# Attention heads of a fused transformer kernel: who splits the negated maxima and who normalises the outputs

## The chip, the cores and the metric

One NeuronCore of a Trainium2 chip runs the whole program. The metric is the device time of one execution, in microseconds (us). The engines are TensorE (PE, matrix products and transpositions), VectorE (DVE), ScalarE (ACT), GpSimd (POOL) and SyncE (SP, which issues transfers).

## What is computed

The program is two transformer layers with a layer norm behind each block. The change touches only the first attention, on 4 sequences of 1024 rows of 128, with 16 heads of 8 columns:

```python
q = split_heads(embedding @ Wq + bq)
k = split_heads(embedding @ Wk + bk)
v = split_heads(embedding @ Wv + bv)
scale = 1.0 / np.sqrt(HDIM)
scores = jnp.einsum('bhqd,bhkd->bhqk', q, k) * scale
attn = jax.nn.softmax(scores, axis=-1)
av = jnp.einsum('bhqk,bhkd->bhqd', attn, v)
```

The softmax needs the maximum of every row of scores. Behind it stand a projection with a norm, a window attention with two layers and feed-forward blocks, a second attention and a last feed-forward block; they are about 1300 of the 2100 us and stay as they are.

## The kernel before

`phase_l0_heads` works in 32 **units**: a unit `n` is one head and one half `z` (512 query columns) of all 4 sequences. Every unit has 8 groups `g` of 128 keys, and every group two half steps `k`. Three units are in work at once:

- For unit `n + 2` (`after2`), TensorE forms plain scores (`cross`, line 433), 32 tiles of 128 rows by 512 columns a unit, two in each half step, into a ring of three PSUM banks `pX`. VectorE takes the maximum of each (`top`, L554) and folds the two halves of each row together with a change of sign (`fold`, L559) at the unit's end. The result `neg` is 128 x 16.
- For unit `n + 1` (`after`), TensorE transposes `neg` in group 1 (`turn_neg`, L441) into a bank of the same ring. `split_neg` writes it as two bf16 rows, the rounded value (L566) and the remainder (L568), and SyncE stores them as two more rows of the operand `Q`, so that the score product of the unit subtracts the maximum.
- For unit `n`, TensorE forms the scores transposed, less the maximum (`score_and_cross`, L448), into two PSUM buffers `pS`; ScalarE takes the exponential (L537); TensorE multiplies by the values (`products`, L465, eight of 32 x 256 a half step) into the one buffer `pO`, with a column of ones that gives the sum.
- For unit `n - 1` (`before`), ScalarE copies `pO` to `O` in group 1 (`take_sums`, L530), TensorE transposes it at the end of group 3 (`close`, L476, four transpositions, again in a bank of the ring), and `norm` on VectorE takes reciprocals of the sums (L576) and multiplies (L580).

Order on each engine is the order of the code, and all dependencies are semaphores. TensorE forms two `cross` tiles beside the two score tiles of each half step, on different rows of the array, and then products. The ring decides how far it runs ahead of VectorE: class `Banks` hands out the three banks in turn; the second number that `take` returns, `back`, says how many maxima may still be missing when a bank is written again. Since VectorE read the transposed tiles in its own order, one counter, `topped`, freed all banks. The first products of a unit wait until `O` has been copied (`o_ready`), since `pO` is single.

The first two units' maxima are formed before unit 0. The loop over units 1 to 24 is a hardware loop of 8 units, taken three times; units 25 to 31 are written out. Units 30 and 31 have no maxima to form. GpSimd only copied values for a head to come (L417). The next phase, `phase_project_norm`, starts behind a barrier of all engines.

## Time and profile before

| | |
|---|---|
| time of 3 runs, median (lowest to highest) | 2095.55 us (2095.2 to 2096.95) |
| the profiled execution, time / span | 2095.52 us / 2093.5 us |
| heads, from the first maximum to the last product of `norm` | 64.4 to 777.6 us |
| PE / DVE / ACT / POOL busy, of the span | 80% / 80% / 56% / 33% |
| the same from 300 to 400 us, within the heads | PE 97.3, DVE 98.2, ACT 81.3, POOL 0.8 of 100 us |
| granted clock of TensorE from 300 to 400 us | 1.00 (2.4 GHz) |

A row of a timeline merges equal instructions that follow each other; the length of such a row is from its first start to its last end. An instruction of an engine may start before the one ahead has ended. A matmul's end is modelled. "Idle before" is the engine's idle time ahead of the row, with the instruction that ended it.

### The profile page before, as it was taken

The page shows a single profiled execution, that of the slowest core. Times are in us where ns is not written, and L with a number is a line of the kernel's source. Part 1 is how long each engine was busy: PE and PEld are TensorE (multiplying, and loading weights), DVE is VectorE, ACT ScalarE, POOL GpSimd, SP SyncE. Part 2 cuts the span into 40 slices and gives each one's busy share as a digit, 9 for nine tenths or more (in the row PEclk, how much of TensorE's full clock was granted, in tenths as well). Part 3 has the DMA queues.
Part 4 walks back from the last instruction along what each step waited for, and adds up shares of the span by engine and source line. Part 5 has one row for each costly group of instructions (what it writes and reads, how often), then busy time and mean ns, then how long its engine had stood idle before and what let it go on. Part 6 is the DMA issues. An engine that isn't in the chain of part 4 may idle for free. (4 is left out here: it accounts for less than half of the span.)

```text
span 2093.5 us, 47784 instructions
## 1 busy us (share of the span) xinstructions
PE 1681.3 (80%) x15985; PEld 891.1 (43%) x15985; DVE 1676.9 (80%) x3448; ACT 1169.1 (56%) x2316; POOL 697.4 (33%) x531
## 2 busy tenths in 40 slices
PE   5799999999999983788888595888885752676768
PEld 3123322323232323455555362655554432565645
DVE  6799999999999916799999464999995778677546
ACT  4078878877888871577777322777775210332411
POOL 3000000000000003788888224888884333223101
PEclk9589999999999996999999897999998975887879
DMA  5200000000010004000000222000001231010022
GB/s 167 62 8 26 17 18 22 27 18 17 20 29 2 2 16 126 16 20 20 22 19 17 56 81 68 21 20 22 19 19 42 77 87 30 2 30 21 22 73 70
DMA packets 144154, 75.92 MB, mean 36 GB/s; under 512 B 53186, under 2 KB 138876, under 8 KB 143740
## 3 DMA queue, kind: packets, MB, share of 16 engines
q1 hardware_dynamic: 133444, 69.13, 11.8%
q10 hardware_dynamic: 10552, 4.70, 0.9%
q8 instruction: 98, 1.61, 0.3%
q14 instruction: 60, 0.49, 0.1%
HBM read 52.54 MB, written 20.98 MB: 35 GB/s over the span
## 5 line engine op out<-in xcount | busy, mean ns | idle before, releaser
L554 DVE TENSOR_REDUCE hd_top<-hd_pX 128x1 f32<-128x512 f32 x1024 | 620.2, 677 | 26.5 <-PE hd_pX L433 26.2
L537 ACT ACTIVATE hd_E<-hd_pS 128x1024 f32<-128x1024 f32 x512 | 524.3, 1024 | 194.5 <-PE hd_pS L448 177.6
L433 PE MATMUL hd_pX<-l_K,l_Q 48*128 48x512 bf16 x1024 | 353.9, 403 | 23.1 <-DMA l_Q<-q_parts 21.6
L465 PE MATMUL hd_pO<-hd_E,l_V 128*32 128x256 f32 x4096 | 330.7, 395 | 16.5 <-ACT hd_O L530 16.3
L448 PE MATMUL hd_pS<-l_Q,l_K 50*128 50x512 bf16 x1024 | 317.6, 387 | 8.7 <-issue 6.5
L1026 ACT ACTIVATE w_E<-w_pS,w_nb,w_inv_q 128x128 f32<-128x128 f32 x512 | 227.9, 459 | 38.0 <-DVE w_nb L1170 38.0
L1089 POOL TENSOR_TENSOR w_inv<-w_ss,w_mhalf 128x16 f32<-128x16 f32 x64 | 186.2, 2910 | 118.1 <-DVE w_ss L1150 118.1
L417 POOL COPY l_V<-l_v_all 128x256 f32 x12 | 4.8, 400 | 557.0 <-PE hd_pO L465 557.0
L465 PEld LDWEIGHTS hd_pO<-hd_E,l_V 128*32 128x32 f32 x4096 | 82.1, 108 | 170.5 <-issue 107.6
L448 PEld LDWEIGHTS hd_pS<-l_Q,l_K 50*128 50x128 bf16 x1024 | 61.6, 94 | 206.0 <-issue 199.0
L433 PEld LDWEIGHTS hd_pX<-l_K,l_Q 48*128 48x128 bf16 x1024 | 89.3, 94 | 125.3 <-DVE hd_top L554 97.5
L921 PE MATMUL w_pQK<-w_wqkv,w_HT 128*128 128x512 f32 x256 | 133.4, 645 | 10.6 <-DVE w_N L1127 9.9
L1012 ACT ACTIVATE w_SQ<-w_pQK 128x1024 f32<-128x1024 f32 x64 | 65.5, 1023 | 121.5 <-PE w_pQK L921 121.5
L1181 DVE TENSOR_TENSOR w_E<-w_E,w_rec 128x512 f32<-128x512 f32 x128 | 117.8, 921 | 4.4
L1026 ACT ACTIVATION_READ_ACCUMULATOR w_E<-w_pS,w_nb,w_inv_q 128x1 f32 x512 | 104.8, 205 | 0.0
L936 PE MATMUL w_pS<-w_ident,w_C 128*128 128x128 f32 x512 | 68.1, 276 | 45.1 <-issue 39.2
L1127 DVE TENSOR_TENSOR w_N<-w_pQK,w_tab 128x256 f32<-128x256 f32 x256 | 94.5, 408 | 0.0
L1077 POOL TENSOR_TENSOR w_C<-w_C,w_N 128x512 f32<-128x512 f32 x64 | 91.1, 1424 | 0.0
L977 PEld LDWEIGHTS w_pO<-w_ET,w_VA 128*64 128x64 f32 x1024 | 59.3, 138 | 74.7 <-issue 73.6
L1682 POOL TENSOR_TENSOR la_QQ<-la_QR 128x4096 f32<-128x4096 f32 x8 | 57.2, 7152 | 99.3 <-PE la_pF L1774 51.5
L1389 ACT ACTIVATE f_G<-f_pG,f_own 128x512 f32<-128x512 f32 (+1 forms) x48 | 32.7, 685 | 102.9 <-PE f_pU L1357 102.8
L1145 DVE TENSOR_REDUCE w_sums<-w_SQ 128x16 f32<-128x1024 f32 x64 | 77.3, 1207 | 14.3 <-ACT w_SQ L1012 14.3
(205 smaller groups left out, 3281.9 us busy)
## 6 DMA issues: line engine op xcount, KB each, us to landing
l_Q<-q_parts SPq DMA_DIRECT2D x192, 32.0 KB
l_K<-k_parts SPq DMA_DIRECT2D x180, 32.0 KB
m<-w_Y SPq DMA_DIRECT2D x64, 64.0 KB, 1.6
f_H<-m SPq DMA_DIRECT2D x32, 128.0 KB
f_X<-m SPq DMA_DIRECT2D x16, 256.0 KB, 3.0
q_parts<-pj_ptq SPq DMA_DIRECT2D x8, 384.0 KB
k_parts<-pj_ptk SPq DMA_DIRECT2D x8, 384.0 KB, 2.5
pj_X<-in_L_attn_embedding_dram SPq DMA_DIRECT2D x8, 256.0 KB, 3.4
```

The source lines that it names most:

```text
L433: nc.tensor.matmul(pX[slot][:, :], Q[m.j][rows, m.z, b, t * P:(t + 1) * P], K[m.j][rows, b, k * 512:(k + 1) * 512], start=True, stop=True) ...
L448: last = nc.tensor.matmul(pS[k][:, b, :], K[n.j][rows, b, g * P:(g + 1) * P], Q[n.j][rows, n.z, b, :], start=True, stop=True)
L465: last = nc.tensor.matmul(pO[VW * b:VW * b + VW, cols], V[n.j][:, b * NT + g, :], E[g % SLOTS][:, b, cols], start=(g == 0 and half == 0), ...
L537: nc.scalar.activation(E[g % SLOTS][:, 2 * k:2 * k + 2, :], pS[k][:, :, :], ACT.Exp).then_inc(exped[k], 1)
L554: nc.vector.tensor_reduce(top2[m.z][:, ROW_ORDER[q], k:k + 1], pX[slot][:, :], AX.X, ALU.max).then_inc(topped, 1)
L921: last = nc.tensor.matmul(pQK[:, z, :], HT[:, t.u, :], wqkv[:, z * INNER:(z + 1) * INNER], start=True, stop=True)
L1026: last = nc.scalar.activation(E[:, r, p, :], pS[t.u][:, r, p, :], ACT.Exp, bias=nb[:, t.u, i:i + 1], scale=inv_q[:, t.u, h:h + 1], accum_o ...
L1077: nc.gpsimd.tensor_tensor(C[:, t.u, 1, :], C[:, t.u, 1, :], N[:, 1, :], ALU.add).then_inc(k_added, 1)
L1089: nc.gpsimd.tensor_tensor(inv[:, :], ss[:, :], mhalf[:, :], ALU.pow).then_inc(inv_ready, 1)
L1127: last = nc.vector.tensor_tensor(sin[:, :, mine], src[:, :, other], ts[:, :, mine].broadcast_to([P, WH, half_d]), ALU.mult)
L1145: nc.vector.tensor_reduce(sums[:, :], SQ[:, :, :].rearrange("p z (h d) -> p (z h) d", h=WH), AX.X, ALU.add).then_inc(summed, 1)
L1181: nc.vector.tensor_tensor(e, e, rec[:, sl].rearrange("p (h a) -> p h a", a=1).broadcast_to([P, PAIRS, P]), ALU.mult)\
```

## The change

VectorE keeps only the maxima and the fold. GpSimd splits `neg` before it is transposed (`part_neg`): it rounds to bf16 into `high` by a product with ones, copies that back to f32 and subtracts it, so that `neg2` holds two times 16 columns. TensorE transposes the 32 columns at once, and ScalarE copies the 32 rows as bf16 (`take_neg`) to `negp`, whose layout changes from 16 rows of two to 32 rows. ScalarE also copies the transposed outputs to SBUF (`take_out`, a new tile `OS`), and GpSimd does the normalisation from there, with the reciprocal as a power of -1. The copies of the values move behind it on GpSimd. A bank that held a transposed tile is now freed by ScalarE's copy (`neg_split`, `o_taken`), and `Banks` tells the waiting side what the bank held.

```diff
-        negp = [s.sb(f"negp{j}", [ROWS, MAX_ROWS, P], BF16) for j in range(2)]
+        high = [s.sb(f"high{j}", [P, ROWS], BF16) for j in range(2)]
+        neg2 = [s.sb(f"neg2_{j}", [P, MAX_ROWS, ROWS]) for j in range(2)]
+        negp = [s.sb(f"negp{j}", [MAX_ROWS * ROWS, P], BF16) for j in range(2)]
         O = s.sb("O", [P, HQ])
+        OS = s.sb("OS", [P, HQ])
         inv = s.sb("inv", [P, QT, B])
+        ones = s.sb("ones", [P, 1])
+        minus = s.sb("minus", [P, 1])
...
+                self.at, self.last = 0, ["top"] * RING
+
+            def take(self, kind="top"):
+
+                gap = RING - 1 if self.at in (0, 1) else RING
+                slot, held = self.at % RING, self.last[-gap]
+                back = gap - 1 - sum(k != "top" for k in self.last[len(self.last) - gap:])
                 self.at += 1
-                self.close = RING if special else max(0, self.close - 1)
-                return slot, back
+                self.last.append(kind)
+                return slot, held, back
...
                 load(sp, 0, 0, Q, q_parts, 0)
                 sp.dma_start(ident[:, :], ident_d).then_inc(ident_in, 16)
@@ -410,15 +420,59 @@
             def _(pool):
                 for h in range(R):
...
+                nc.gpsimd.memset(ones[:, :], 1.0).then_inc(constants, 1)
+                nc.gpsimd.memset(minus[:, :], -1.0).then_inc(constants, 1)
+                pool.wait_ge(constants, 2)
+
+                def part_neg(m):
+
+                    pool.wait_ge(folded[m.z], m.h + 1)
+                    pool.wait_ge(neg_turned[m.z], m.h)
+                    one = ones[:, :].broadcast_to([P, ROWS])
+                    nc.gpsimd.tensor_tensor(high[m.z][:, :], neg[m.z][:, :], one, ALU.mult).then_inc(neg_high, 1)
+                    pool.wait_ge(neg_high, m.n + 1)
+                    nc.gpsimd.tensor_tensor(neg2[m.z][:, 0, :], high[m.z][:, :], one, ALU.mult)
+                    nc.gpsimd.tensor_tensor(neg2[m.z][:, 1, :], neg[m.z][:, :], high[m.z][:, :], ALU.subtract).then_inc(neg_parted[m.z], 1)
+
+                def norm(n):
+                    pool.wait_ge(o_taken, n.n + 1)
+                    pool.wait_ge(normed, n.n)
+                    sums = OS[:, :].rearrange("p (t b c) -> p t b c", t=QT, b=B)
+                    power = minus[:, :].rearrange("p (t b) -> p t b", t=1).broadcast_to([P, QT, B])
+                    nc.gpsimd.tensor_tensor(inv[:, :, :], sums[:, :, :, HD], power, ALU.pow).then_inc(inverted, 1)
+                    pool.wait_ge(inverted, n.n + 1)
+                    out = attn[:, :, bass.ds(n.h * HD, HD)].rearrange("p (b z t) d -> p z t b d", b=B, z=2)[:, n.z]
+                    scale = inv[:, :, :].rearrange("p t (b a) -> p t b a", a=1).broadcast_to([P, QT, B, HD])
+                    nc.gpsimd.tensor_tensor(out, sums[:, :, :, 0:HD], scale, ALU.mult).then_inc(normed, 1)
+
+                def unit(n, before, after, after2):
+                    if after.exists():
+                        part_neg(after)
+                    if not n.is_first():
+                        norm(before)
+                    if n.z == 0 and not n.is_first() and (n.known is None or n.known // 2 - 1 + R < H):
+                        h = before.h + R
+                        nc.gpsimd.tensor_copy(V[before.j][:, :, 0:HD], v_all[:, :, bass.ds(h * HD, HD)]).then_inc(v_ready[before.j], 1)
+
+                part_neg(Unit(0, 0))
+                units(pool, unit)
+                norm(Unit(0, UNITS - 1))
 
...
+
+                    slot, held, back = banks.take(kind)
+                    if held == "neg":
+                        pe.wait_ge(neg_split[turned[0].z], turned[0].h + 1)
+                    elif held == "out":
+                        pe.wait_ge(o_taken, turned[1].n + 1)
+                    elif not isinstance(tops, int) or tops > back:
+                        pe.wait_ge(topped, tops - back)
+                    return pX[slot]
...
-                    nc.tensor.transpose(pX[slot][0:ROWS, 0:P], neg[m.z][:, :], ident[:, :]).then_inc(neg_turned[m.z], 1)
+                    pe.wait_ge(neg_parted[m.z], m.h + 1)
+                    px = bank("neg", tops)
+                    nc.tensor.transpose(px[0:MAX_ROWS * ROWS, 0:P], neg2[m.z][:, :, :].rearrange("p r c -> p (r c)"), ident[:, :])\
+                        .then_inc(neg_turned[m.z], 1)
+                    turned[0] = m
...
                         if g == 3 and not n.is_first():
-                            if not after2.exists():
-                                if after.exists():
-                                    pe.wait_ge(neg_split[after.z], after.h + 1)
-                                else:
-                                    pe.wait_ge(normed, before.n)
                             close(before, tops)
...
-                pe.wait_ge(normed, UNITS - 1)
...
+
+                def take_neg(m):
+                    act.wait_ge(neg_turned[m.z], m.h + 1)
+                    if m.known is None or m.known > 1:
+                        act.wait_ge(neg_stored[m.z], NEGS * m.h)
+                    slot, _, _ = banks.take("neg")
+                    nc.scalar.copy(negp[m.z][:, :], pX[slot][0:MAX_ROWS * ROWS, 0:P]).then_inc(neg_split[m.z], 1)
+
+                def take_out(n):
+                    act.wait_ge(o_turned, n.n + 1)
+                    act.wait_ge(normed, n.n)
+                    slot, _, _ = banks.take("out")
+                    nc.scalar.copy(OS[:, :], pX[slot][:, :]).then_inc(o_taken, 1)
+
...
-                units(act, unit)
+                        if after2.exists():
+                            pass_tops(TOPS // NT)
+                        if g == 1 and after.exists():
+                            take_neg(after)
+                        if g == 3 and not n.is_first():
+                            take_out(before)
+
+                pass_tops(TOPS)
+                take_neg(Unit(0, 0))
+                pass_tops(TOPS)
+                units(act, unit, banks)
                 take_sums(Unit(0, UNITS - 1))
+                take_out(Unit(0, UNITS - 1))
...
                 def fold(m):
                     dve.wait_ge(topped, TOPS * (m.n + 1))
-                    dve.wait_ge(neg_turned[m.z], m.h)
+                    dve.wait_ge(neg_parted[m.z], m.h)
                     nc.vector.tensor_reduce(neg[m.z][:, :], top2[m.z][:, :, :], AX.X, ALU.max, negate=True).then_inc(folded[m.z], 1)
-
...
-                def split_neg(m):
-                    slot, _ = banks.take(True)
-                    turned = pX[slot][0:ROWS, 0:P]
-                    dve.wait_ge(neg_turned[m.z], m.h + 1)
-                    dve.wait_ge(neg_stored[m.z], NEGS * m.h)
-                    nc.vector.tensor_copy(negp[m.z][:, 0, :], turned).then_inc(neg_high, 1)
-                    dve.wait_ge(neg_high, m.n + 1)
-                    nc.vector.tensor_tensor(negp[m.z][:, 1, :], turned, negp[m.z][:, 0, :], ALU.subtract)\
-                        .then_inc(neg_split[m.z], 1)
-
-                def norm(n):
-                    slot, _ = banks.take(True)
-                    dve.wait_ge(o_turned, n.n + 1)
-                    dve.wait_ge(normed, n.n)
-                    sums = pX[slot][:, :].rearrange("p (t b c) -> p t b c", t=QT, b=B)
-                    nc.vector.reciprocal(inv[:, :, :], sums[:, :, :, HD]).then_inc(inverted, 1)
-                    dve.wait_ge(inverted, n.n + 1)
-                    out = attn[:, :, bass.ds(n.h * HD, HD)].rearrange("p (b z t) d -> p z t b d", b=B, z=2)[:, n.z]
-                    scale = inv[:, :, :].rearrange("p t (b a) -> p t b a", a=1).broadcast_to([P, QT, B, HD])
-                    nc.vector.tensor_tensor(out, sums[:, :, :, 0:HD], scale, ALU.mult).then_inc(normed, 1)
...
                     if m.n == 0:
-                        split_neg(m)
+                        banks.take("neg")
...
                         if g == 1 and after.exists():
-                            split_neg(after)
+                            banks.take("neg")
                         if g == 3 and not n.is_first():
-                            norm(before)
+                            banks.take("out")
...
-                norm(Unit(0, UNITS - 1))
```

Two places show the instructions in their order. **VectorE**, from the start of the phase to the end of unit 0 (`hd_top_0`, `hd_top_1` are the maxima of the two halves `z`), before:

```order
L554 TENSOR_REDUCE hd_top_0<-hd_pX 128x1 x32
L559 TENSOR_REDUCE hd_neg<-hd_top_0 128x16
L566 CAST hd_negp<-hd_pX 16x128
L568 TENSOR_TENSOR hd_negp<-hd_pX,hd_negp 16x128
L554 TENSOR_REDUCE hd_top_1<-hd_pX 128x1 x32
L559 TENSOR_REDUCE hd_neg<-hd_top_1 128x16
L554 TENSOR_REDUCE hd_top_0<-hd_pX 128x1 x8
L566 CAST hd_negp<-hd_pX 16x128
L568 TENSOR_TENSOR hd_negp<-hd_pX,hd_negp 16x128
L554 TENSOR_REDUCE hd_top_0<-hd_pX 128x1 x24
L559 TENSOR_REDUCE hd_neg<-hd_top_0 128x16
```

and now:

```order
L629 TENSOR_REDUCE hd_top_0<-hd_pX 128x1 x32
L634 TENSOR_REDUCE hd_neg<-hd_top_0 128x16
L629 TENSOR_REDUCE hd_top_1<-hd_pX 128x1 x32
L634 TENSOR_REDUCE hd_neg<-hd_top_1 128x16
L629 TENSOR_REDUCE hd_top_0<-hd_pX 128x1 x32
L634 TENSOR_REDUCE hd_neg<-hd_top_0 128x16
```

The cast and the subtraction have gone from between the maxima. In later units the reciprocal and the product have gone from behind the sixteenth maximum in the same way.

**ScalarE**, one unit of the loop from its group 1 to its group 4 (`hd_E` exponentials, `hd_O` the copied sums, `hd_OS` the transposed ones), before:

```order
L536 REGISTER_ALU
L537 ACTIVATE hd_E<-hd_pS 128x1024
L530 COPY hd_O<-hd_pO 128x512
L537 ACTIVATE hd_E<-hd_pS 128x1024
L536 REGISTER_ALU
L537 ACTIVATE hd_E<-hd_pS 128x1024 x2
L536 REGISTER_ALU
L537 ACTIVATE hd_E<-hd_pS 128x1024 x2
L534 REGISTER_ALU
```

and now:

```order
L601 REGISTER_ALU
L602 ACTIVATE hd_E<-hd_pS 128x1024
L577 COPY hd_O<-hd_pO 128x512
L602 ACTIVATE hd_E<-hd_pS 128x1024
L580 REGISTER_ALU
L582 REGISTER_ALU
L584 CAST hd_negp<-hd_pX 32x128
L601 REGISTER_ALU
L602 ACTIVATE hd_E<-hd_pS 128x1024 x2
L601 REGISTER_ALU
L602 ACTIVATE hd_E<-hd_pS 128x1024 x2
L590 COPY hd_OS<-hd_pX 128x512
```

A cast of the transposed maxima now stands behind the exponentials of group 1, and a copy of the transposed outputs behind those of group 3.

## Rows read from the trace of the kernel before

**Rows 1.** Timeline of VectorE over one unit (start us, length us, engine, line, operation, count, [idle before <- what ended it]):
```profile
318.34 4.87 DVE L554 TENSOR_REDUCE hd_top<-hd_pX 128x1 f32<-128x512 f32 x8
323.25 0.28 DVE L566 CAST hd_negp<-hd_pX 16x128 bf16<-16x128 f32 x1
...
323.77 4.85 DVE L554 TENSOR_REDUCE hd_top<-hd_pX 128x1 f32<-128x512 f32 x8
...
329.14 9.64 DVE L554 TENSOR_REDUCE hd_top<-hd_pX 128x1 f32<-128x512 f32 x16
338.82 0.19 DVE L559 TENSOR_REDUCE hd_neg<-hd_top 128x16 f32<-128x32 f32 x1
338.92 4.87 DVE L554 TENSOR_REDUCE hd_top<-hd_pX 128x1 f32<-128x512 f32 x8
...
359.50 0.19 DVE L559 TENSOR_REDUCE hd_neg<-hd_top 128x16 f32<-128x32 f32 x1
```

**Rows 2.** Timeline of TensorE over the same unit:
```profile
319.08 0.39 PE L433 MATMUL hd_pX<-l_K,l_Q 48*128 48x512 bf16 x1
...
322.37 0.64 PE L465 MATMUL hd_pO<-hd_E,l_V 128*32 128x256 f32 x8 [0.51 <-ACT hd_O L530]
322.94 0.28 PE L441 MATMUL hd_pX<-hd_ident,hd_neg 128*16 128x128 f32 x1
...
323.15 0.39 PE L433 MATMUL hd_pX<-l_K,l_Q 48*128 48x512 bf16 x1
...
324.50 0.39 PE L433 MATMUL hd_pX<-l_K,l_Q 48*128 48x512 bf16 x1
...
325.60 0.39 PE L448 MATMUL hd_pS<-l_Q,l_K 50*128 50x512 bf16 x1
...
326.71 0.39 PE L448 MATMUL hd_pS<-l_Q,l_K 50*128 50x512 bf16 x1
...
328.41 0.39 PE L433 MATMUL hd_pX<-l_K,l_Q 48*128 48x512 bf16 x1
```

**Rows 3.** Timeline of ScalarE over the same unit:
```profile
321.53 0.58 ACT L530 COPY hd_O<-hd_pO 128x512 f32<-128x512 f32 x1
...
323.78 2.19 ACT L537 ACTIVATE hd_E<-hd_pS 128x1024 f32<-128x1024 f32 x2 [0.75 <-PE hd_pS L448]
...
329.04 1.02 ACT L537 ACTIVATE hd_E<-hd_pS 128x1024 f32<-128x1024 f32 x1 [0.67 <-PE hd_pS L448]
```

**Rows 4.** Timeline of TensorE in the two units without maxima:
```profile
740.17 0.64 PE L465 MATMUL hd_pO<-hd_E,l_V 128*32 128x256 f32 x8 [0.75 <-ACT hd_O L530]
...
759.44 0.64 PE L465 MATMUL hd_pO<-hd_E,l_V 128*32 128x256 f32 x8 [0.75 <-ACT hd_O L530]
```

**Rows 5.** Timeline of VectorE, first and last fold of the unit loop:
```profile
127.68 0.19 DVE L559 TENSOR_REDUCE hd_neg<-hd_top 128x16 f32<-128x32 f32 x1
...
736.39 0.18 DVE L559 TENSOR_REDUCE hd_neg<-hd_top 128x16 f32<-128x32 f32 x1
```

**Rows 6.** Timeline of TensorE, first score product of unit 0:
```profile
105.40 0.61 PE L448 MATMUL hd_pS<-l_Q,l_K 50*128 50x512 bf16 x1 [2.13 <-DMA l_Q<-hd_negp]
```

**Rows 7.** Groups by line and form (busy us, mean ns | idle before), GpSimd, then ScalarE:
```profile
L1089 POOL TENSOR_TENSOR w_inv<-w_ss,w_mhalf 128x16 f32<-128x16 f32 x64 | 186.2, 2910 | 118.1 <-DVE w_ss L1150 118.1
...
L1083 POOL TENSOR_TENSOR w_C<-w_C,w_inv 128x512 f32<-128x512 f32 x64 | 66.7, 1042 | 9.5 <-POOL w_C L1077 0.4
...
L1096 POOL TENSOR_TENSOR w_inv_q<-w_inv,w_ones 128x8 f32<-128x8 f32 x64 | 27.0, 422 | 10.5 <-POOL w_VA L1068 10.2
...
L1007 ACT COPY w_HT<-w_pV 128x128 f32<-128x128 f32 x64 | 17.0, 265 | 71.1 <-PE w_pV L914 71.1
```

**Rows 8.** Timeline of VectorE at the end of the heads:
```profile
777.02 0.26 DVE L576 RECIPROCAL hd_inv<-hd_pX 128x16 f32<-128x16 f32 x1 [11.32 <-PE hd_pX L476]
777.31 0.29 DVE L580 TENSOR_TENSOR l_attn<-hd_pX,hd_inv 128x128 f32<-128x128 f32 x1
```

**Rows 9.** Timeline of GpSimd inside the unit of rows 1:
```profile
321.44 0.40 POOL L417 COPY l_V<-l_v_all 128x256 f32 x1 [45.42 <-PE hd_pO L465]
```

More of the change, by code:

```diff
@@ L297, in phase_l0_heads @@
         neg_high = s.sem("neg_high")
+        neg_parted = s.sems("neg_parted")
+        constants = s.sem("constants")
         neg_split = s.sems("neg_split")
@@ L412, in _ @@
                     nc.gpsimd.tensor_copy(V[h][:, :, 0:HD], v_all[:, :, h * HD:h * HD + HD]).then_inc(v_ready[h], 1)
-                with pool.Fori(1, H // R) as i:
-                    for j in range(R):
-                        h = R * i + j
-                        pool.wait_ge(summed[LAST], 2 * (NT // SLOTS) * (h - R + 1))
-                        nc.gpsimd.tensor_copy(V[j][:, :, 0:HD], v_all[:, :, bass.ds(h * HD, HD)]).then_inc(v_ready[j], 1)
+                nc.gpsimd.memset(ones[:, :], 1.0).then_inc(constants, 1)
@@ L421, in _, with bank @@
                 banks = Banks()
+                turned = [None, None]
+                def bank(kind, tops):
+                    slot, held, back = banks.take(kind)
[6 more added lines that the diff above has]
+                    return pX[slot]
                 def cross(m, q, k):
@@ L429, in cross @@
                         pe.wait_ge(loaded[m.j], LOADS * (m.round + 1))
-                    slot, back = banks.take()
-                    if m.known != 0 or 2 * q + k > back:
-                        pe.wait_ge(topped, TOPS * m.n + 2 * q + k - back)
-                    nc.tensor.matmul(pX[slot][:, :], Q[m.j][rows, m.z, b, t * P:(t + 1) * P],
+                    px = bank("top", TOPS * m.n + 2 * q + k)
+                    nc.tensor.matmul(px[:, :], Q[m.j][rows, m.z, b, t * P:(t + 1) * P],
                                      K[m.j][rows, b, k * 512:(k + 1) * 512], start=True, stop=True).then_inc(crossed, 1)
                 def turn_neg(m, tops):
-                    pe.wait_ge(folded[m.z], m.h + 1)
-                    slot, back = banks.take(True)
-                    pe.wait_ge(topped, tops - back)
-                    nc.tensor.transpose(pX[slot][0:ROWS, 0:P], neg[m.z][:, :], ident[:, :]).then_inc(neg_turned[m.z], 1)
+                    pe.wait_ge(neg_parted[m.z], m.h + 1)
[3 more added lines that the diff above has]
+                    turned[0] = m
                 def score_and_cross(n, g, k, m):
@@ L472, in close @@
                     pe.wait_ge(o_ready, n.n + 1)
-                    slot, back = banks.take(True)
-                    pe.wait_ge(topped, tops - back)
+                    px = bank("out", tops)
                     for t in range(QT):
-                        last = nc.tensor.transpose(pX[slot][:, t * P:(t + 1) * P], O[:, t * P:(t + 1) * P], ident[:, :])
+                        last = nc.tensor.transpose(px[:, t * P:(t + 1) * P], O[:, t * P:(t + 1) * P], ident[:, :])
                     last.then_inc(o_turned, 1)
+                    turned[1] = n
                 for m in (Unit(0, 0), Unit(0, 1)):
@@ L501, in unit @@
                         if g == 1 and after.exists():
-                            if not after2.exists():
-                                pe.wait_ge(normed, before.n)
                             turn_neg(after, tops)
                         if g == 3 and not n.is_first():
-                            if not after2.exists():
-                                if after.exists():
-                                    pe.wait_ge(neg_split[after.z], after.h + 1)
-                                else:
-                                    pe.wait_ge(normed, before.n)
                             close(before, tops)
@@ L524, in _ @@
             def _(act):
+                banks = Banks()
                 load(act, 0, 0, K, k_parts, 1)
@@ L530, in take_sums, with pass_tops @@
                     nc.scalar.copy(O[:, :], pO[:, :]).then_inc(o_ready, 1)
+                def take_neg(m):
[9 more added lines that the diff above has]
+                    nc.scalar.copy(OS[:, :], pX[slot][:, :]).then_inc(o_taken, 1)
+                def pass_tops(count):
+                    for _ in range(count):
+                        banks.take()
                 def unit(n, before, after, after2):
@@ L551, in top @@
                     for k in range(2):
-                        slot, _ = banks.take()
+                        slot, _, _ = banks.take()
                         dve.wait_ge(crossed, TOPS * m.n + 2 * q + k + 1)
```

10 lines of the change are left out of this document (4 added, 6 removed).

## Prediction, made before the changed kernel ran

> **What bounds the kernel now.** I read the table of busy time first, then the timeline of each engine over one unit in the middle of the heads, since the change touches only this phase. VectorE is the busiest engine there, and its timeline shows a chain without holes [rows 1]: 8 maxima, the split, 8 maxima, the normalisation, 16 maxima, the fold, and the next unit. The unit lasts 338.92 - 318.34 = 20.58 us. A maximum takes 0.68 us, but starts follow each other sooner: (9.64 - 0.68)/15 = 0.597 us. So 32 maxima are 19.12 us, and 1.46 us are other work, by the starts in the rows: the split costs 323.77 - (318.34 + 8 x 0.597) = 0.65, the normalisation 329.14 - (323.77 + 4.78) = 0.59, the fold 338.92 - (329.14 + 9.56) = 0.22. The next unit is longer by 0.1 (359.50 - 338.82 = 20.68), and they go on in pairs, 20.63 on average. Between the first and the last fold of the loop lie 29 units in 608.71 us [rows 5]; 29 x 20.63 is 598.2, and the other 10.5 us are two longer units, at the two backward branches.
>
> The second thing to read is how far behind VectorE the next engine is. In the two units that have no maxima, TensorE has nothing to wait for but ScalarE's copy of the sums, and such a unit takes 759.44 - 740.17 = 19.27 us, with 0.75 us of wait in it [rows 4]. VectorE after the change has 19.12 + 0.22 = 19.34 us of work. The two are equal within 0.1 us, and only three banks lie between them, so neither number is the new unit: each time TensorE makes a pause, VectorE will run dry. What the change brings has to be walked through at these pauses.
>
> **The split, in group 1.** Let S be the start of a unit's first maximum (318.34). TensorE's path to the ninth tile is fixed to S: the second tile of the second half step waits for a bank that the first maximum frees (319.08, S + 0.74, the first maximum's 0.68 and a handoff) [rows 2]; from there run products, scores, an exponential, the copy of the sums at S + 3.19 [rows 3], products at S + 4.03, which waited 0.51 us for that copy, the transposition at S + 4.60 and the ninth tile at S + 4.81 [rows 2]. Nothing of this was on VectorE's split, so it stays. A tile of 0.39 us and a handoff of 0.03 later the ninth maximum can start: S + 5.23. Today it starts at S + 5.43 (323.77), in every second unit at S + 5.53. So of the 0.65 us that VectorE is spared, 0.20 or 0.30 is gained, and the rest becomes a wait for TensorE.
>
> **The normalisation, in group 3.** TensorE needs 1.11 us for a half step when it is free (326.71 - 325.60). Today its two half steps from 323.15 to 325.60 take 2.45, because the tile at 324.50 waits for the maximum behind the split [rows 2]. That bank held the transposed maxima; now ScalarE's copy frees it, by about S + 5.2, and the wait goes: 2.21, a gain of 0.24. Then the seventeenth tile comes 328.41 - 323.15 - 0.25 = 5.01 us behind the ninth, and so does the seventeenth maximum behind the ninth: 5.01 where today it is 329.14 - 323.77 = 5.37. VectorE alone would need 8 x 0.597 = 4.78, so 0.23 is again a wait. Gain 0.36.
>
> **The rest of the unit** has 16 maxima and the fold, 9.78 us, on VectorE as before. TensorE regains 0.09 us in each half step (1.20 against 1.11) and is a full ring ahead again within four. The new unit is 5.23 + 5.01 + 9.78 = 20.02 us, in both halves z. Gain 20.63 - 20.02 = **0.61 us a unit**. In 29 units this is 17.7 us. The two long units are bound by TensorE in their first part and gain perhaps half: I take 17.2. Unit 0 and the two units without maxima gain nothing.
>
> **ScalarE's two copies.** Both fall into gaps. It idles 0.75 us before the exponential at 323.78 and 0.67 before that at 329.04 [rows 3], in both cases while TensorE does the transposition and the next scores. A copy of 128 x 128 from PSUM takes 0.27 us [rows 7], and the cast of 32 rows should be nearest to it; bounds 0.2 to 0.58, a whole copy of 512 columns. It can start at S + 4.90, with the exponential due at S + 5.44. The copy of the outputs is a second one of 0.58 us [rows 3], of which the engine is taken for 0.46 (the next exponential starts 0.46 to 0.47 behind it). It can start when the four transpositions end, 0.5 us ahead of the exponential. It fits with nothing to spare. I cost both at nothing; if this cover is gone, each delays the scores and with them the ring.
>
> **GpSimd** takes three operations of 128 x 16 for the split: 0.42 us each, by the 128 x 8 product [rows 7], so about 1.4 us with handoffs, of the 4.6 between the fold and the transposition. Normalising costs a power of 128 x 16, 2.91 us as in the window attention, and a product of 128 x 128, between 0.42 and 1.04 us [rows 7], 0.57 by the line between them. All this is some 5 us in a unit of 20 and nobody waits for it, save at both ends of the phase.
>
> **The start.** TensorE now waits for GpSimd's split before the second set of maxima, some 0.9 us net. Unit 0 starts when the transfer of the negated maxima has landed, and TensorE waits 2.13 us for it [rows 6]; that transfer stands behind loads in SyncE's queue, which don't depend on this. Cost nothing.
>
> **The end.** Behind the last transposition stand now a reciprocal and a product, done by 777.60, 0.58 us from the first start [rows 8]. Then come the barrier and the next phase. Now there will be a copy of 0.58, the power of 2.91, the product of 0.57 and 0.15 of handoffs, 4.2 us: **3.6 us** more, with nothing to hide it, since all engines wait at the barrier. Lower bound, with the power at the price of the smallest product, 0.42: 1.1.
>
> A rule of the Trainium skill bears on this. The power on GpSimd takes 2.91 us against 0.26 for the reciprocal on VectorE [rows 7, 8], eleven times as much. The Trainium skill, GPSIMD Engine Reference, section 3.1, has GpSimd 1.96 times slower than VectorE in an elementwise operation. By that the two operations would take 1.96 x 0.55 = 1.1 us and the total would come out some 2.4 us lower; the row decides, since it is this very operation and shape.
>
> Would GpSimd slow VectorE? A copy of 128 x 256 on GpSimd ran at 321.44 to 321.84 [rows 9], within the first 8 maxima of the unit, which took 4.87 us, as did those of the next unit without one [rows 1]. So no.
>
> **Sum**, against the profiled execution's own 2095.52 us, which is the median of the runs (2095.55): -17.2 + 3.6 = -13.6, so 2082 us.
>
> **Rivals.**
> 1. *VectorE's work simply goes.* If TensorE's lead carried it over the pauses, the unit would be 19.34: 29 x 1.29 = 37.4 less, 3.6 more, 2062 us. For it speaks that VectorE has no hole today; against it that the ninth tile is late by the path through the copy of the sums, which hangs on the first maximum and not on the split. Chance 0.08.
> 2. *The cast gets in the way.* If it takes 0.5 us or more, or starts late, the exponential of group 2 slips by 0.3 to 0.5 us, and the products and banks behind it. Net gain 0.1 to 0.3 a unit, 3 to 9 us, less 3.6: 2090 to 2096 us. Chance 0.12.
> 3. *Both copies land on the path* (slower). ScalarE feeds TensorE from two score buffers. If both copies delay the exponentials by their whole length, 0.27 + 0.58 = 0.85 us a unit, the unit is 0.24 longer than today: +7.0 + 3.6, 2106 us. It decides from 0.61 - 3.6/29 = 0.49 us of delay a unit. Against it stand both idle gaps. Chance 0.08.
> 4. *The change doesn't spare VectorE.* The order of instructions shows that it does; no chance.
>
> **How the numbers follow.** The forecast has a chance of 0.72, with its own range from 2076 (gain 0.75 a unit, end 1.1 to 3.6) to 2088 (gain 0.4). Adding rival 2 gives 0.84 within 2076 to 2095; I widen below to 2075, as both long units could gain the full 0.61. A measurement of this kernel can tell 0.2%, 4.2 us, from no change. Faster by more: the forecast, rival 1, a little of rival 2: 0.82. Within: most of rival 2, 0.10. Slower: rival 3, 0.08.
>
> **What would show it.** Right: from fold to fold 20.0 us; VectorE idle 0.4 us before the ninth and 0.2 before the seventeenth maximum, ended by TensorE's tile; ScalarE's cast about 0.27; about 5 us from the last transposition to the barrier, most of it GpSimd's power. Wrong: a unit of 19.4 (rival 1) or over 20.3 (2); exponentials right behind a copy without a gap, with TensorE waiting for them (3); maxima slower than 0.60 us apart while GpSimd works.

## The result, and the profile after

The changed kernel takes **2085.64 us** in the median of 4 runs (2085.04 to 2087.73) against 2096.25 for the kernel before in the same session (2095.2 to 2101.09): a ratio of 0.9947, with a 95% interval from 0.9929 to 0.9964, so 7.5 to 14.9 us less. Measured again later it was 2082.2 in the median of five runs, against 2097.3 for the kernel before in that session, a ratio of 0.9931 (0.9914 to 0.9948); a sixth run, at a granted clock of 0.79 instead of 0.91, took 2144.2 and is left out. The forecast was 2082, the range 2075 to 2095.

Busy time of the changed kernel, from its page (us, share of the span, instructions):

```profile
PE 1669.2 (80%) x15985; PEld 888.9 (43%) x15985; DVE 1651.5 (79%) x3320; ACT 1196.1 (57%) x2380; POOL 822.1 (39%) x693
```

Before, VectorE had 1676.9 us, ScalarE 1169.1 and GpSimd 697.4. VectorE lost 25.4 us of busy time, 0.79 us in each of 32 units, and ScalarE and GpSimd took its work over. What became of that shows only in the timeline. VectorE of the changed kernel, two units, in the columns of [rows 1]:

```profile
315.33 4.88 DVE L629 TENSOR_REDUCE hd_top<-hd_pX 128x1 f32<-128x512 f32 x8
320.58 4.88 DVE L629 TENSOR_REDUCE hd_top<-hd_pX 128x1 f32<-128x512 f32 x8 [0.37 <-PE hd_pX L485]
325.63 9.67 DVE L629 TENSOR_REDUCE hd_top<-hd_pX 128x1 f32<-128x512 f32 x16 [0.17 <-PE hd_pX L485]
335.33 0.19 DVE L634 TENSOR_REDUCE hd_neg<-hd_top 128x16 f32<-128x32 f32 x1
335.44 4.87 DVE L629 TENSOR_REDUCE hd_top<-hd_pX 128x1 f32<-128x512 f32 x8
340.68 4.88 DVE L629 TENSOR_REDUCE hd_top<-hd_pX 128x1 f32<-128x512 f32 x8 [0.37 <-PE hd_pX L485]
345.73 9.67 DVE L629 TENSOR_REDUCE hd_top<-hd_pX 128x1 f32<-128x512 f32 x16 [0.17 <-PE hd_pX L485]
355.43 0.19 DVE L634 TENSOR_REDUCE hd_neg<-hd_top 128x16 f32<-128x32 f32 x1
355.61 1.29 DVE L629 TENSOR_REDUCE hd_top<-hd_pX 128x1 f32<-128x512 f32 x2
```

In [rows 1] four pieces of other work stood between the maxima and no hole. Now only the fold is left, and there are two holes, 0.37 us before the ninth and 0.17 before the seventeenth maximum, both ended by TensorE's tile (L485). The parts are 5.25 + 5.05 + 9.81 = 20.11 us in one unit and 5.24 + 5.05 + 9.88 = 20.17 in the next. From fold to fold the mean is 20.14 where it was 20.63: 0.49 us gained.

TensorE over the first part of that unit, S = 315.33, to be read against [rows 2]:

```profile
316.08 0.39 PE L485 MATMUL hd_pX<-l_K,l_Q 48*128 48x512 bf16 x1
...
319.36 0.64 PE L518 MATMUL hd_pO<-hd_E,l_V 128*32 128x256 f32 x8 [0.50 <-ACT hd_O L577]
319.93 0.28 PE L492 MATMUL hd_pX<-hd_ident,hd_neg 128*32 128x128 f32 x1
...
320.15 0.39 PE L485 MATMUL hd_pX<-l_K,l_Q 48*128 48x512 bf16 x1
...
324.61 0.66 PE L528 MATMUL hd_pX<-hd_ident,hd_O 128*128 128x128 f32 x4
...
325.20 0.39 PE L485 MATMUL hd_pX<-l_K,l_Q 48*128 48x512 bf16 x1
...
326.41 0.39 PE L485 MATMUL hd_pX<-l_K,l_Q 48*128 48x512 bf16 x1
```

The second tile starts at S + 0.75, the products that waited for ScalarE's copy of the sums at S + 4.03, the transposition (L492) at S + 4.60 and the ninth tile at S + 4.82. These are the distances of before to 0.01 us: TensorE's path didn't change, and VectorE now waits for it. The tile at 326.41 is the third behind the transposed outputs (L528) and the first that needs their bank again.

ScalarE over the same stretch, against [rows 3]:

```profile
320.25 0.26 ACT L584 CAST hd_negp<-hd_pX 32x128 bf16<-32x128 f32 x1 [0.22 <-PE hd_pX L492]
320.79 4.34 ACT L602 ACTIVATE hd_E<-hd_pS 128x1024 f32<-128x1024 f32 x4 [0.28 <-PE hd_pS L501]
325.30 0.59 ACT L590 COPY hd_OS<-hd_pX 128x512 f32<-128x512 f32 x1 [0.17 <-PE hd_pX L528]
325.83 1.02 ACT L602 ACTIVATE hd_E<-hd_pS 128x1024 f32<-128x1024 f32 x1
```

The cast (L584) lies wholly in the idle time before the exponential, with 0.28 us to spare. The copy (L590) runs into the next exponential, but that starts 0.63 us behind the tile at 325.20, as it did before (329.04 and 328.41, [rows 2, 3]), so the copy doesn't delay it. It ends at 325.89, 0.52 us ahead of the tile at 326.41 that needs its bank.

The phase as a whole: first and last fold of the loop, in VectorE's timeline (against [rows 5]):

```profile
128.61 0.19 DVE L634 TENSOR_REDUCE hd_neg<-hd_top 128x16 f32<-128x32 f32 x1
...
722.54 0.19 DVE L634 TENSOR_REDUCE hd_neg<-hd_top 128x16 f32<-128x32 f32 x1
```

and the end of the heads in the timelines of ScalarE, GpSimd and SyncE's queue, whose transfer is the first of the next phase:

```profile
763.15 0.59 ACT L590 COPY hd_OS<-hd_pX 128x512 f32<-128x512 f32 x1 [0.74 <-PE hd_pX L528]
...
763.81 2.90 POOL L442 TENSOR_TENSOR hd_inv<-hd_OS,hd_minus 128x16 f32<-128x16 f32 x1 [8.49 <-ACT hd_OS L590]
766.79 0.41 POOL L446 TENSOR_TENSOR l_attn<-hd_OS,hd_inv 128x128 f32<-128x128 f32 x1
...
769.03 0.38 SPq L698 DMA_DIRECT2D po_ident<-in_ident_dram  x1
```

Fold to fold is 593.93 us, where it was 608.71: 14.8 less, of which 12.4 lie in 27 units and 2.3 in the two long ones (25.25 and 26.49 us before, 25.14 and 24.26 after). The 27 don't all gain 0.49: the last five, which are written out behind the hardware loop, went from 20.53 to 20.15 (the first of the five from 20.82 to 20.44), some 0.38 each. From the last fold to the next phase it is 46.49 where it was 42.70: 3.8 more. The first fold comes 0.9 later, since TensorE stayed at its lower clock (granted 0.5, which is 1.2 GHz) until 117.5 us instead of 115.2 before it rose; in four other runs with the same instructions up to there the first fold came at 126.99 to 128.08, so most of this isn't the change. The sum is -14.8 + 0.9 + 3.8 = -10.1 us at the end of the heads. The later phases have the same code, and in this execution took 2.6 us more; it was the slowest of its four.

### The profile page after: what moved, and what is told of

The parts are those of the page before. It is cut to its first block and busy times, and to the rows that moved or that the text cites. A ratio compares the mean times of both kernels' runs of the same rounds, so it can differ in the third digit from the quotient of the medians.

```text
span 2086.0 us, 47974 instructions
## 1 busy us (share of the span) xinstructions
PE 1669.2 (80%) x15985; PEld 888.9 (43%) x15985; DVE 1651.5 (79%) x3320; ACT 1196.1 (57%) x2380; POOL 822.1 (39%) x693
## 5 line engine op out<-in xcount | busy, mean ns | idle before, releaser
L485 PE MATMUL hd_pX<-l_K,l_Q 48*128 48x512 bf16 x1024 | 355.5, 403 | 23.1 <-DMA l_Q<-q_parts 21.7
L501 PE MATMUL hd_pS<-l_Q,l_K 50*128 50x512 bf16 x1024 | 313.3, 387 | 7.3 <-issue 5.9
L442 POOL TENSOR_TENSOR hd_inv<-hd_OS,hd_minus 128x16 f32<-128x16 f32 x32 | 92.9, 2902 | 327.8 <-ACT hd_OS L590 327.8
L501 PEld LDWEIGHTS hd_pS<-l_Q,l_K 50*128 50x128 bf16 x1024 | 57.2, 94 | 205.0 <-issue 193.7
L485 PEld LDWEIGHTS hd_pX<-l_K,l_Q 48*128 48x128 bf16 x1024 | 90.5, 93 | 118.6 <-DVE hd_top L629 83.9
L432 POOL TENSOR_TENSOR hd_high<-hd_neg,hd_ones 128x16 bf16<-128x16 f32 x32 | 7.0, 217 | 247.6 <-DVE hd_neg L634 218.3
```

The costliest lines, as they stand in the source:

```text
L442: nc.gpsimd.tensor_tensor(inv[:, :, :], sums[:, :, :, HD], power, ALU.pow).then_inc(inverted, 1)
L485: nc.tensor.matmul(px[:, :], Q[m.j][rows, m.z, b, t * P:(t + 1) * P], K[m.j][rows, b, k * 512:(k + 1) * 512], start=True, stop=True).then_ ...
L501: last = nc.tensor.matmul(pS[k][:, b, :], K[n.j][rows, b, g * P:(g + 1) * P], Q[n.j][rows, n.z, b, :], start=True, stop=True)
```

## The experiments

In each, the ratio is to the kernel before on the same chip in the same session (medians 2096.7 to 2097.3 us), "unit" is the mean from fold to fold over an even and an odd regular unit of the hardware loop, and the end is the time from the last fold to the first transfer of the next phase. The kernel before has 20.63 and 42.70 us, the changed one 20.14 and 46.49 (46.23 when run again).

**One half of the change alone.** *e_split_only* has the new split; VectorE still normalises, and ScalarE's copy of the outputs goes too. Against the changed kernel, on GpSimd and on VectorE:

```diff
-                    if not n.is_first():
-                        norm(before)
...
                         if g == 3 and not n.is_first():
-                            banks.take("out")
+                            norm(before)
```

> Only the split leaves VectorE; the normalisation stays there as in the kernel before. Theory (the gain is what TensorE's path leaves at each pause): the ninth maximum starts 5.25 us behind the first, as in the changed kernel, not 5.43; the normalisation starts when the sixteenth maximum is read, and its 0.6 us are added, so from the ninth to the seventeenth maximum it takes about 5.4 to 5.5 us. Unit 20.35 us, about 0.25 less than before; 29 units give 7 us, no long end, 2088 to 2090 us. Rival (VectorE's saved work counts in full): unit 20.63 - 0.65 = 19.98, 2077 us.

Measured: 2091.2 us, 0.9965 (0.9952 to 0.9979), unit 20.46, end 42.44. VectorE:

```profile
317.64 4.88 DVE L626 TENSOR_REDUCE hd_top<-hd_pX 128x1 f32<-128x512 f32 x8
322.89 4.88 DVE L626 TENSOR_REDUCE hd_top<-hd_pX 128x1 f32<-128x512 f32 x8 [0.37 <-PE hd_pX L483]
327.69 0.25 DVE L638 RECIPROCAL hd_inv<-hd_pX 128x16 f32<-128x16 f32 x1
328.07 0.29 DVE L642 TENSOR_TENSOR l_attn<-hd_pX,hd_inv 128x128 f32 x1
328.28 9.65 DVE L626 TENSOR_REDUCE hd_top<-hd_pX 128x1 f32<-128x512 f32 x16
337.96 0.19 DVE L631 TENSOR_REDUCE hd_neg<-hd_top 128x16 f32<-128x32 f32 x1
```

The ninth maximum stands at 5.25, but the seventeenth another 5.39 behind it, as in [rows 1]: the normalisation is still on the path, and of the split's 0.65 us only 0.17 are gained. I had put it at 0.28, but my own terms, 5.25 and at least 5.4 with the remaining 9.78, already add up to 20.43 and not to 20.35. The rest, 0.03 us, is that in every second unit the first maximum starts 0.18 us behind the fold and not 0.11 (below).

*e_norm_only* is the other half: GpSimd normalises, VectorE still splits the transposed maxima, from 16 rows as before. Against the changed kernel, on the same two engines:

```diff
-                    if after.exists():
-                        part_neg(after)
...
                         if g == 1 and after.exists():
-                            banks.take("neg")
+                            split_neg(after)
```

> Only the normalisation leaves VectorE; the split stays there as in the kernel before. Theory: the ninth maximum keeps its 5.43 us behind the first, and the tile that waits for the maximum behind the split may still wait; from the ninth to the seventeenth maximum about 5.05 us instead of 5.37. Unit 20.3 us, 0.3 less than before; 29 x 0.3 = 9 us less, the end 3.8 us more: 2090 to 2091 us. Rival (full): unit 20.63 - 0.59 = 20.04, 2095.5 - 17 + 3.8 = 2082 us. The two partial gains should add up to about the 0.48 us a unit that the whole change brought.

Measured: 2093.6 us, 0.9981 (0.9968 to 0.9993), unit 20.31, end 45.91. VectorE:

```profile
321.06 4.85 DVE L625 TENSOR_REDUCE hd_top<-hd_pX 128x1 f32<-128x512 f32 x8
326.08 9.67 DVE L625 TENSOR_REDUCE hd_top<-hd_pX 128x1 f32<-128x512 f32 x16 [0.17 <-PE hd_pX L481]
```

Ninth to seventeenth maximum are 5.02 us with a wait of 0.17, as in the whole change. The gains add up: 0.17 + 0.32 = 0.49. So each half is cut off by its own pause of TensorE, and neither hid the other's gain.

**Does GpSimd's long operation cost anything inside the units?** *e_mult_for_power* multiplies by -1 where the power stood, so the outputs aren't divided by their sums; everything else stays.

```diff
-                    nc.gpsimd.tensor_tensor(inv[:, :, :], sums[:, :, :, HD], power, ALU.pow).then_inc(inverted, 1)
+                    nc.gpsimd.tensor_tensor(inv[:, :, :], sums[:, :, :, HD], power, ALU.mult).then_inc(inverted, 1)
```

> The changed kernel with a product by -1 in the place of the power of -1 on GpSimd, so the outputs are not divided by their sums. It takes 2.7 us from GpSimd in every unit. Theory (GpSimd is waited for only at the end): the unit stays 20.15 us and the end is shorter by 2.7 us, 2083 us. Rival (GpSimd's work slows VectorE's maxima, whose pace was 0.600 against 0.597 us): unit shorter by up to 0.1, another 2 to 3 us, 2080 us.

Measured: 2083.0 us, 0.9936 (0.9924 to 0.9949), unit 20.14, end 43.54. The group of that line in the page of the changed kernel (busy us, mean ns of one | idle before):

```profile
L442 POOL TENSOR_TENSOR hd_inv<-hd_OS,hd_minus 128x16 f32<-128x16 f32 x32 | 92.9, 2902 | 327.8 <-ACT hd_OS L590 327.8
```

and in the page of this one:

```profile
L442 POOL TENSOR_TENSOR hd_inv<-hd_OS,hd_minus 128x16 f32<-128x16 f32 x32 | 7.1, 222 | 333.8 <-ACT hd_OS L590 333.8
```

2.68 us of GpSimd's time went from every unit and the unit didn't move; 2.95 us went from the end (2.69 against the repeated run's 46.23), where it stands alone.

*e_last_norm_vector* takes only the end: the last unit is normalised on VectorE from the bank.

```diff
                 units(pool, unit)
-                norm(Unit(0, UNITS - 1))
...
                 take_sums(Unit(0, UNITS - 1))
-                take_out(Unit(0, UNITS - 1))
...
                 units(dve, unit, banks)
+                n = Unit(0, UNITS - 1)
+                slot, _, _ = banks.take("out")
...
+                nc.vector.reciprocal(inv[:, :, :], sums[:, :, :, HD]).then_inc(inverted, 1)
...
+                nc.vector.tensor_tensor(out, sums[:, :, :, 0:HD], scale, ALU.mult).then_inc(normed, 1)
```

> The changed kernel, but VectorE normalises the last unit straight from PSUM as the kernel before did, with no copy by ScalarE. Theory: the end comes back to that of the kernel before, 3.8 us less, 2082 us. Rival (part of the longer end was hidden by the code of the next phase being loaded): 1 to 2 us less.

Measured: 2083.4 us, 0.9932 (0.992 to 0.9945), unit 20.14, end 42.51. The 3.8 us at the end are thus the price of ScalarE's copy and GpSimd's two operations, and they go when VectorE does the last unit. In the time of the whole program this step is too small to be told from none.

**How much cover do ScalarE's copies have?** *e_copy_three_times* copies the transposed outputs twice more:

```diff
                     slot, _, _ = banks.take("out")
+                    nc.scalar.copy(OS2[:, :], pX[slot][:, :])
+                    nc.scalar.copy(OS3[:, :], pX[slot][:, :])
                     nc.scalar.copy(OS[:, :], pX[slot][:, :]).then_inc(o_taken, 1)
```

> The changed kernel with two more copies of the transposed outputs to tiles that nobody reads, which puts 0.93 us more on ScalarE in each unit ahead of the exponential of group 4. Theory (ScalarE has 4 us to spare a unit and catches up): the exponential is late by 0.9, a score step by 0.2 to 0.3, and the unit grows by 0.3 us at most, under 9 us in all: 2086 to 2094. Rival (the copies lie on the path, my rival 3): 0.93 x 31 = 29 us more, 2114 us, and then the one copy would cost about 14 us in the changed kernel.

Measured: 2099.1 us, 1.0019 (1.0008 to 1.003), unit 20.65. ScalarE's last copy, then TensorE behind the transposed outputs:

```profile
329.39 0.60 ACT L593 COPY hd_OS<-hd_pX 128x512 f32<-128x512 f32 x1
```

```profile
328.65 0.39 PE L486 MATMUL hd_pX<-l_K,l_Q 48*128 48x512 bf16 x1
...
329.54 0.39 PE L502 MATMUL hd_pS<-l_Q,l_K 50*128 50x512 bf16 x1
...
330.05 0.39 PE L486 MATMUL hd_pX<-l_K,l_Q 48*128 48x512 bf16 x1
```

and VectorE at the same place:

```profile
328.76 1.29 DVE L632 TENSOR_REDUCE hd_top<-hd_pX 128x1 f32<-128x512 f32 x2 [0.17 <-PE hd_pX L486]
330.48 1.89 DVE L632 TENSOR_REDUCE hd_top<-hd_pX 128x1 f32<-128x512 f32 x3 [0.43 <-PE hd_pX L486]
```

0.95 us more on ScalarE cost 0.51 a unit, more than the 0.3 I had allowed and less than the 0.93 of the rival. The reason isn't a late exponential. The one behind the copies does come 0.91 us late, at 329.87, but the next score tile (L502, 329.54) doesn't wait for it. It is the bank: the third tile behind the transposition, which otherwise starts with that score tile, waits until ScalarE lets go of it (copies from 328.44 to 329.99, tile at 330.05, 0.51 late), and VectorE runs dry for 0.43 us more. The whole gain of the change is gone. The one copy of the changed kernel does have cover: its bank is free 0.52 us ahead of the tile that needs it, less 0.06 for the handoff, and 0.95 - 0.46 is about the 0.51 measured.

**Can TensorE's pause be moved away?** The products that wait 0.50 us for the copy of the sums stand ahead of the transposition. *e_after_late_products* puts them half a step later, and *e_before_late_products* makes the same edit in the kernel before:

```diff
                         score_and_cross(n, g, 0, after2)
+                        if g == 2:
+                            products(n, 0, 0)
...
-                        if g > 0:
+                        if g > 1:
                             products(n, g - 1, 0)
```

> The changed kernel with the first products of a unit one half step later, behind the first scores of group 2, so that TensorE does not stand idle until ScalarE has copied the sums. Theory (the wait for the copied sums is what makes VectorE run dry): TensorE's 0.5 us of wait goes, the ninth maximum starts at the pace of VectorE, 4.8 us behind the first, TensorE's unit without maxima is 18.5 us, and the unit with them is VectorE's 19.34 plus little: 19.4 to 19.6. 29 x 0.6 = 17 less than the changed kernel, about 2068 us. Rival (the transposition itself, or VectorE's pace, sets the ninth maximum): unit stays 20.1, 2085 us.

Measured: 2090.9 us, 0.9968 (0.9956 to 0.998), unit 20.43, 0.3 longer than without it. VectorE:

```profile
317.95 6.07 DVE L633 TENSOR_REDUCE hd_top<-hd_pX 128x1 f32<-128x512 f32 x10
324.63 3.68 DVE L633 TENSOR_REDUCE hd_top<-hd_pX 128x1 f32<-128x512 f32 x6 [0.61 <-PE hd_pX L485]
```

and TensorE:

```profile
321.68 0.28 PE L492 MATMUL hd_pX<-hd_ident,hd_neg 128*32 128x128 f32 x1 [0.21 <-DVE hd_top L633]
...
322.28 0.39 PE L485 MATMUL hd_pX<-l_K,l_Q 48*128 48x512 bf16 x1
...
322.88 0.39 PE L485 MATMUL hd_pX<-l_K,l_Q 48*128 48x512 bf16 x1 [0.21 <-DVE hd_top L633]
323.20 1.07 PE L518 MATMUL hd_pO<-hd_E,l_V 128*32 128x256 f32 x16
```

The wait for the sums is gone and the ninth maximum comes without a hole. But now the transposition itself and the second tile behind it each wait 0.21 us for a maximum: of three banks the transposition holds one, so TensorE can't run ahead. Then come 1.07 us of products in one piece, and VectorE runs dry for 0.61 before the eleventh maximum. The pause was moved and not removed.

> The kernel before with the same later products and nothing else. Theory: VectorE has 19.12 + 0.22 + 0.6 + 0.6 = 20.5 us of work in a unit of 20.63 and stays the bound, so the unit falls only to 20.4 to 20.5, 3 to 6 us less: 2090 to 2092 us. Then the change's sparing of VectorE is worth far more with the later products than without: some 1 us a unit. Rival (the wait for the sums costs each kernel the same): 20.63 - 0.6, 2078 us.

Measured: 2096.5 us, 0.9997 (0.9988 to 1.0006), unit 20.67: no gain, a miss as well. The ninth maximum comes 5.30 us behind the first instead of 5.43 or 5.53, but the seventeenth 5.57 behind the ninth instead of 5.37: here too the pause was moved. *e_both* has two of the edits shown above, the late products and the last unit on VectorE:

> Later first products and the last normalisation on VectorE together. If both effects are what I take them for, they add up: 17 + 3.8 us less than the changed kernel, about 2064 us. If the later products bring nothing, 2082 us.

Measured: 2090.6 us, 0.9964 (0.9951 to 0.9977), unit 20.42, end 40.94, where *e_after_late_products* has 20.43 and 44.67. The two effects stand side by side.

**Does it depend on where the transposition stands?** *f_after_again* is the changed kernel once more, as a base for the runs that follow (2082.2 us, 0.9931, above). *f_late_turn* transposes the maxima in group 5 instead of group 1, away from the pause for the sums, and `take_neg` and VectorE's step over the bank go with it:

```diff
-                        if g == 1 and after.exists():
+                        if g == 5 and after.exists():
                             turn_neg(after, tops)
```

> The changed kernel with the transposition of the negated maxima and ScalarE's cast in group 5 instead of group 1. Theory (VectorE runs dry where TensorE's pause meets a ring that has just lost a bank or has no lead; in group 5 the lead is back): the ninth maximum starts at 5.03 us behind the first instead of 5.25, the wait before the seventeenth stays 0.2, and the pause of 0.21 in group 5 is covered. Unit 19.9 us, 29 x 0.22 = 6 us less than the changed kernel, 2079 us. Rival (each pause costs its length wherever it stands): unit stays 20.14, 2085.6 us.

Measured: 2090.2 us, 0.9966 (0.9953 to 0.9979), unit 20.20, and six units of 20.5 to 21.0, two in each round of the hardware loop, in which TensorE waits up to 0.8 us for the store of the maxima, which now starts later. The loop is 5.1 us longer than in *f_after_again*. VectorE, group 5 of one unit and the start of the next:

```profile
326.34 6.08 DVE L629 TENSOR_REDUCE hd_top<-hd_pX 128x1 f32<-128x512 f32 x10 [0.17 <-PE hd_pX L485]
332.60 0.69 DVE L629 TENSOR_REDUCE hd_top<-hd_pX 128x1 f32<-128x512 f32 x1 [0.18 <-PE hd_pX L485]
...
336.42 4.87 DVE L629 TENSOR_REDUCE hd_top<-hd_pX 128x1 f32<-128x512 f32 x8
341.45 4.88 DVE L629 TENSOR_REDUCE hd_top<-hd_pX 128x1 f32<-128x512 f32 x8 [0.16 <-PE hd_pX L485]
346.50 6.08 DVE L629 TENSOR_REDUCE hd_top<-hd_pX 128x1 f32<-128x512 f32 x10 [0.17 <-PE hd_pX L485]
```

and TensorE in that group 5:

```profile
330.43 0.28 PE L492 MATMUL hd_pX<-hd_ident,hd_neg 128*32 128x128 f32 x1
...
330.68 0.39 PE L485 MATMUL hd_pX<-l_K,l_Q 48*128 48x512 bf16 x1
...
331.28 0.39 PE L485 MATMUL hd_pX<-l_K,l_Q 48*128 48x512 bf16 x1
```

First to ninth maximum is 5.03 us, which I had worked out, 0.22 less. But group 5, where nothing was late before, now has the same hole: the tile behind the transposition starts at 330.68, the next only at 331.28, where 0.23 us lie between two tiles elsewhere, and 332.60 - (326.34 + 10 x 0.597) = 0.28 us are lost: more than the 0.22 gained. *f_late_turn_tail* adds the edit of *e_last_norm_vector*:

> The same with the last unit normalised on VectorE. Both theories: 3.8 us less than the one without it; with the theory above 2075 us, with its rival 2082 us.

Measured: 2089.2 us, 0.9954 (0.9941 to 0.9968), unit 20.20, end 42.56. Only the end changed, by 3.7 us; the medians of the two runs are too near each other to show it.

*f_late_all* joins all three edits, the late transposition, the late products and the last unit on VectorE:

> As the last one, and with the first products a half step later too. That move made the unit longer by 0.3 us when the transposition stood right behind it, because TensorE then waited twice for a bank with one of three held, and the double products came behind these waits. Theory (the held bank did it): with the transposition gone from there the tiles of group 2 wait for one bank less, VectorE runs dry by about 0.1 us instead of 0.6, unit 19.7 to 19.8, 2070 to 2072 us. Rival (the double products alone did it): unit 20.2 or more, 2082 us or above.

Measured: 2081.6 us, 0.9925 (0.991 to 0.994), unit 20.11, again without the six units (20.2 to 20.8) that wait for the store. VectorE:

```profile
335.17 9.76 DVE L631 TENSOR_REDUCE hd_top<-hd_pX 128x1 f32<-128x512 f32 x16
345.16 6.07 DVE L631 TENSOR_REDUCE hd_top<-hd_pX 128x1 f32<-128x512 f32 x10 [0.23 <-PE hd_pX L484]
351.41 0.69 DVE L631 TENSOR_REDUCE hd_top<-hd_pX 128x1 f32<-128x512 f32 x1 [0.18 <-PE hd_pX L484]
```

16 maxima now run in one piece: first to seventeenth maximum 9.99 us, against 10.30 in the changed kernel, 10.59 with the late products alone and 10.08 with the late transposition alone (346.50 - 336.42). So the late products cost 0.29 with the transposition in front of them and gain 0.09 without it; that bears out the theory of the held bank, but most of the 0.31 comes from the moved transposition. And 0.28 goes again in group 5, and the 19.7 to 19.8 us of my expectation weren't reached. It has the lowest median of all complete kernels; from the changed one of the same session (0.9931) it can't be told.

## Why the prediction was right, and where it was off

**The bound of a unit** was right. VectorE looked full, and the forecast said it would run dry for 0.4 and 0.2 us before the ninth and the seventeenth maximum; the rows show 0.37 and 0.17, ended by TensorE. So of 1.24 us that VectorE was spared, 0.49 were gained, and rival 1 (19.34 us a unit) is out. The two halves tried alone confirm the division, with 0.17 and 0.32.

**The mis-sized term** is the gain of a unit, 0.61 in the forecast and 0.49 in the trace. In the split's part it is 0.02 (5.25 for 5.23). In the normalisation's part it is 0.04: the seventeenth tile comes 325.20 - 320.15 = 5.05 behind the ninth, 5.01 was worked out, because the half step ahead of the transposed outputs takes 1.14 us and not the 1.11 of a free one. The largest piece, 0.06, is in the part that I had taken over unchanged as 9.78: it takes 9.81 in one unit and 9.88 in the next. The first maximum behind the fold starts 0.11 us after it in one unit and 0.18 in the next. That it alternates goes with the split on GpSimd: *e_split_only* has it too, and *e_norm_only*, with the split on VectorE, has 0.10 or 0.11 in both. By which wait it comes no run showed.

**The two long units** gained 2.3 us together, more than the half gain that I gave them, and most of that is luck. Their length goes with the time that TensorE spends at the lower clock (granted 0.5) behind the loop's branch: in the second one that was 10.2 us before (unit 26.49) and 3.4 in the changed kernel (unit 24.26). Over all runs such a unit took 24.0 to 27.9 us. The loop gained 14.8 where 17.2 was forecast; by the regular unit alone 3.5 were missing, and the clock gave some of it back.

**ScalarE's copies**, costed at nothing, did cost nothing measurable. The cast took 0.255 us, near the 0.265 taken, so rival 2, which needed 0.5, didn't come. "Fits with nothing to spare" was right of the second copy as seen from the exponential: ScalarE could take that from 0.47 us behind the copy's start, 325.77, and it starts at 325.83. What the forecast didn't see is the way in which a longer copy costs: rivals 2 and 3 let it delay the exponentials, but by the run with three copies it is the bank of the ring that comes late, and for the bank the one copy has 0.46 us to spare.

**GpSimd.** The three operations of the split took 0.22 us each, where I took 0.42 from a product of 128 x 8 in another phase; nobody waits for them. The power took 2.90 us (2.91 forecast), the product 0.41 (0.57). That they slow nobody in the units was forecast from one copy, and the run without the power shows it for the power. Without the three operations of the split (*e_norm_only*) the eight maxima beside them take 4.87 us, with them 4.87 or 4.88. The Trainium skill, GPSIMD Engine Reference, section 1, says that GpSimd shares its SBUF interfaces with VectorE and that they contend when VectorE runs in a 2-port mode or has two SBUF inputs. The trace agrees so far as it goes: the maxima read PSUM, and the unit is 20.14 us with 2.90 or with 0.22 us of this operation. With VectorE reading SBUF no run here tried it.

**The end** was right: 3.6 forecast, 3.8 in the profiled execution and 3.5 in the repeated one. The rule of the Trainium skill that was set against it (GPSIMD Engine Reference, section 3.1, 1.96 times slower, stated there for an addition of 2048 columns) gave an estimate of 1.1 us for the two operations; 3.31 were measured. By the rows the product is 0.41 against 0.29 on VectorE, 1.4 times, and the power 2.90 against 0.26 for the reciprocal, 11 times.

**The start** was costed at nothing. The second set of maxima in the prologue does come 0.7 us later, but unit 0 waits for its transfer as before, and its first score product starts at 105.39 us where it was 105.40. The 0.9 us in the sum above come behind that and are in the main a matter of the clock: where it rose at 115.5 in both, the first fold came at 128.08 with the changed code (*e_mult_for_power*) and at 127.88 with that of before (*e_before_late_products*), so up to 0.2 may be the change's.

**What stays open**: the wait behind the 0.07 us in every second unit; why the five units behind the hardware loop gain 0.38 and not 0.49; the 2.6 us of the later phases in one execution; and whether a fourth bank, or transposed maxima in a bank outside the ring, would win back the holes. Neither was tried.

## What to carry to other kernels

When the busiest engine is spared work, count how far behind it the next engine is and walk that engine's path to each point where it has to deliver: the gain is what its pauses leave, here 0.49 of 1.24 us, and it was found by distances of rows, not by shares of busy time. In a small ring of buffers a piece of work that takes one can leave a hole wherever it is put: the transposition, moved away from its hole in group 1, made one of 0.28 us in group 5, where there had been none. And ask of each reader how long it holds its buffer, not only whom it delays on its own engine. Work that is free inside a loop on an idle engine isn't free behind the last round: look there at the price of the whole chain, and give the last round to the fast engine (3.7 to 4.0 us at the end here, too little to show in the time of the whole program).

## What was unexpected in the hardware

- A power of 128 x 16 on GpSimd takes 2.90 us, 13 times a product of the same shape (0.22), so it is the operation and not the size that costs.
- TensorE's stay at the lower clock (granted 0.5) differs between executions of the same code: in four executions with the changed kernel's order of work (one with the product for the power, one with the last unit on VectorE) unit 0 took 21.9 to 23.5 us and the long units 24.3 to 25.7; over all kernels measured here the long units took 24.0 to 27.9. That is as much as an edit of this kind moves.
- Three copies of 128 x 512 from PSUM one behind another on ScalarE start 0.47 to 0.48 us apart though each takes 0.58 to 0.60; the last one's full length still counts for whoever waits for the bank.
